# The left and right side projections of a tile issued in turn, product by product, into two PSUM banks

## The reference

```python
u = jnp.einsum('bid,bjd->bij', h, h) / temper
a = jax.nn.softmax(u, axis=-1)
delta = a * adjacency_matrix
attn = delta / (jnp.sum(delta, axis=-1, keepdims=True) + 1e-10)
hl = h @ wl.T + b_l          # "left"
hs = h @ ws.T + b_s          # "self"
hr = h @ wr.T + b_r          # "right"
ctx = einsum(attn * upper, hl) + diag_a[..., None] * hs + einsum(attn * lower, hr)
o = (ctx - mean) / jnp.sqrt(var + LN_EPS) * g + beta
return (jax.nn.relu(o), None)
```

## Time and profile before

| | |
|---|---|
| time, median of 3 runs | 1282.53 us (1281.9 to 1283.6) |
| the profiled execution's own time | 1282.98 us |
| its span, first to last instruction | 1281.2 us |
| TensorE matmul busy | 1263.4 us, 99% |
| TensorE weight loads busy | 1166.7 us, 91% |
| VectorE busy | 990.4 us, 77% |
| ScalarE busy | 632.6 us, 49% |
| GpSimd busy | 370.6 us, 29% |
| mean granted TensorE clock | 0.996 |
| a full step (gram of layer 1 at 606.53 and at 645.56) | 39.03 us |

### The profile page before, as it was taken

The page is one execution under the profiler, slowest core; times in us unless marked ns, Lnnn a source line. Parts: engine busy times, 40 slices in busy tenths (PEclk is TensorE's granted clock), DMA queues, the critical chain, the costliest instruction groups (busy, mean ns, idle before and its releaser), DMA issues.

```text
span 1281.2 us, 34717 instructions
## 1 busy us (share of the span) xinstructions
PE 1263.4 (99%) x13844; PEld 1166.7 (91%) x13844; DVE 990.4 (77%) x2691; ACT 632.6 (49%) x1338; POOL 370.6 (29%) x401
## 2 busy tenths in 40 slices
PE   9999999999999999999999999999999999999986
PEld 8999999999999999999999999999999999999975
DVE  6777778777878777787778787777877777877877
ACT  6544554544554445545445545455454455454543
POOL 3322323232323222323223232223232232323211
PEclk9999999999999999999999999999999999999989
DMA  8211110111110111110111101111101111011000
GB/s 275 85 39 57 58 57 25 35 57 57 57 57 4 55 57 57 57 28 31 57 58 58 57 15 44 57 57 57 43 16 57 57 58 58 20 39 45 26 14 26
DMA packets 53072, 66.34 MB, mean 52 GB/s; under 512 B 17840, under 2 KB 39856, under 8 KB 52784
## 3 DMA queue, kind: packets, MB, share of 16 engines
q1 hardware_dynamic: 52768, 63.93, 16.5%
q10 hardware_dynamic: 144, 0.20, 0.0%
HBM read 38.54 MB, written 12.58 MB: 40 GB/s over the span
## 4 chain that ended last, share of the span: by engine, by line
PE 97%; DVE 1%; issue 1%; ACT 1%; POOL 0%; POOLq 0%; DVEq 0%; ACTq 0%
PE bank L420 25%; PE bank L422 23%; PE bank L421 23%; PE bank L623 7%; PE bank L569 4%; PE bank L532 4%; PE bank L517 3%; PE bank L498 3%; PE bank L545 2%; PE bank L555 2%; PE bank L603 1%; PE bank L631 0%; DVE probs L1222 0%; POOL probs L1727 0%; PE bank L745 0%
## 5 line engine op out<-in xcount | busy, mean ns | idle before, releaser
L420 PE MATMUL bank<-w_hi,hT_hi 128*128 128x384 f32 x1158 | 405.4, 350 | 0.2 <-ACT hT_hi L1048 0.2
L422 PE MATMUL bank<-w_hi,hT_lo 128*128 128x384 f32 x1158 | 390.3, 337 | 0.0
L421 PE MATMUL bank<-w_lo,hT_hi 128*128 128x384 f32 x1158 | 390.1, 337 | 0.0
L420 PEld LDWEIGHTS bank<-w_hi,hT_hi 128*128 128x128 f32 x1158 | 218.3, 189 | 6.6 <-issue 2.0
L421 PEld LDWEIGHTS bank<-w_lo,hT_hi 128*128 128x128 f32 x1158 | 218.9, 189 | 0.0
L422 PEld LDWEIGHTS bank<-w_hi,hT_lo 128*128 128x128 f32 x1158 | 218.3, 189 | 0.0
L1293 DVE TENSOR_TENSOR hlr<-bank,rows 128x384 f32<-128x384 f32 x256 | 142.3, 557 | 70.9 <-PE bank L422 68.0
L1740 POOL TENSOR_TENSOR ln_rstd<-ln_var,minus_half 128x2 f32<-128x2 f32 x125 | 96.2, 769 | 322.1 <-DVE ln_var L1386 113.8
L1727 POOL TENSOR_TENSOR probs<-probs,row_max 128x768 f32<-128x768 f32 x64 | 94.6, 1478 | 265.7 <-DVE row_max L1228 265.7
L1310 DVE TENSOR_TENSOR late<-bank,rows 128x384 f32<-128x384 f32 x128 | 71.3, 558 | 118.0 <-PE bank L422 117.9
L420 PE MATMUL bank<-xT_hi,w_hi 128*128 128x256 f32 x558 | 158.7, 284 | 0.0
(11 more groups left out here) (131 smaller groups left out, 2370.9 us busy)
## 6 DMA issues: line engine op xcount, KB each, us to landing
v_halves<-v_stage SPq DMA_DIRECT2D x128, 99.0 KB, 2.3
x_in<-in_x SPq DMA_DIRECT2D x32, 384.0 KB, 4.0
xT_in<-in_xT SPq DMA_DIRECT2D x31, 384.0 KB, 3.4
out<-late SPq DMA_DIRECT2D x31, 384.0 KB, 2.4
late<-in_w SPq DMA_DIRECT2D x7, 576.0 KB, 6.5
adj_in<-in_adj SPq DMA_DIRECT2D x32, 96.0 KB, 3.8
adjT_in<-in_adjT SPq DMA_DIRECT2D x64, 48.0 KB, 3.2
rows<-in_vectors SPq DMA_DIRECT2D x1, 1536.0 KB, 8.7
```

Source lines behind the costliest of these rows:

```text
L420: nc.tensor.matmul(o, l_hi, r_hi, start=first and n == 0, stop=False)
L421: nc.tensor.matmul(o, l_hi, r_lo, start=False, stop=False)
L422: done = nc.tensor.matmul(o, l_lo, r_hi, start=False, stop=final and n == last)
```

## The change

`project_side` keeps its waits, which move to a function `side_waits` of their own. `project_sides` first does the waits of both sides of a tile, and then issues the 18 matmuls of the tile in turn, left, right, left, right, each pair with the same stationary part of h. The number of matmuls, their operands, their banks and the order of the terms within each side are as before; where two neighbours had different W parts with the same h part they now have different W matrices and banks.

```diff
-            def project_side(st, l, t, m):
+            def side_waits(st, l, t, m):
                 if st.unit(LATE) == 0 and t == 0 and m == LEFT:
...
                 if t == 1 and m == RIGHT:
 
                     need(pe, e_ready, st.count(LATE, 4, 2 * l + 2))
+
+            def project_side(st, l, t, m):
+                side_waits(st, l, t, m)
                 project_h(st, l, t, m, HLR_BANKS[l][2 * t + m]).then_inc(hlr_psum, 1)
 
             def project_sides(st, l):
+
                 for t in range(T):
                     for m in (LEFT, RIGHT):
-                        project_side(st, l, t, m)
+                        side_waits(st, l, t, m)
+                    for kc in range(KC):
+                        h_hi, h_lo = hT_hi[:, t, kc, :], hT_lo[:, t, kc, :]
+                        for n, (a, part) in enumerate(((h_hi, 0), (h_hi, 1), (h_lo, 0))):
+                            for m in (LEFT, RIGHT):
+                                final = kc == KC - 1 and n == 2
+                                done = nc.tensor.matmul(HLR_BANKS[l][2 * t + m][:, 0:D], a,
+                                                        weight(W_LATE + 3 * l + m, kc)[part],
+                                                        start=kc == 0 and n == 0, stop=final)
+                                if final:
+                                    done.then_inc(hlr_psum, 1)
```

## The result

| | before | after |
|---|---|---|
| median | 1282.40 us (4 runs, 1281.9 to 1283.6) | 1295.41 us (4 runs, 1295.2 to 1295.7) |
| span of the profiled execution | 1281.2 us | 1293.8 us |
| a full step | 39.03 us | 39.45 us |

The changed kernel is slower by a ratio of 1.0100, 95% interval 1.0087 to 1.0113, that is 13.0 us. The forecast was 1294.6 us. The step in the table is read at one place; the mean from gram(0) of the second unit to gram(0) of the 31st, 29 steps, is 39.04 us before and 39.44 after.

The account below looks back on a forecast made before the run. TensorE, busy 99% of the span, was taken to bound the kernel. 9.6 + 2.2 + 0.3 = 12.1 us on the profiled 1282.98 us gave 1295.1, median 0.45 lower: 1294.6 us, range 1284 to 1305.

Parts of the forecast that it names:

- The products: TensorE's 2,196 products in `project_sides`: interval stays 173.3 ns despite the new order, so 0 us.
- Layer 1: VectorE gets the left side late, delaying h0; TensorE waits 0.32 us at transpose_h in thirty steps, 9.6 us.
- Layer 0: Right side's wait for the context now stands ahead of slot 1: hole of 0.07 us in 31 stages, 2.2 us.
- The first unit: Where VectorE still splits weights, the new order may add up to 0.4 us once; 0.3 us taken.

Follow-up runs that it names:

- run 5: Changed kernel with both edits, right side's waits ahead of slot 2 and statistics of h0 ahead of the left side: 1283.47 us.
- run 1: Sides take turns in layer 1 only, layer 0 as in the kernel before: 1292.28 us, 9.5 over the kernel before.
- run 4: Changed kernel with VectorE's statistics of h0 in layer 1 moved ahead of the left side: 1286.53 us, 3.8 over the kernel before.
- Run 3: Changed kernel with the right side's waits ahead of its first product, slot 2, no longer ahead of slot 1: 1292.29 us.
- runs 2: Sides take turns in layer 0 only, layer 1 as in the kernel before: 1286.34 us, 3.6 over the kernel before.
- Run 8: Changed kernel with one added, unused VectorE addition ahead of the statistics of h0 in layer 1: 1310.31 us.

## Why the prediction was right

- **The products.** Forecast 0 us in place of a gain. Right: 173.4 ns, and run 5 bounds it at 0.4 ns of cost and 0.7 ns of gain. The Trainium skill (TensorE: Matmul & The Clock Gate, Back-to-back issue gap) gives an isolated gap that comes to 162.5 ns for 384 columns. Neither order reaches it here, with 173.3 and 173.4 ns, so the 11 ns between are not the price of accumulating twice running in one bank; what they are, no run shows.
- **Layer 1.** Forecast 0.32 us a step, 9.6 us. Measured 0.32 us a step and 9.5 us (run 1), with each link where it was forecast. Over all thirty steps the trace's mean is 0.31 us, 9.4 us together. It came from the order of VectorE's list: `stats_outer` stood behind two sides that it does not need (run 4).
- **Layer 0.** Forecast 0.07 us in each of 31 stages, 2.2 us. The trace has 0.09 in 29 of them, 0.16 in the last and none in the first unit, which has no context of a unit before to wait for: 2.7 us. The release took 0.12 us, the upper end of the rows used. Run 3 closes it.
- **The first unit.** Forecast 0.3 us and bounded at 0.4, measured 0.9 from its first gram to its second. Of this, 0.8 lie between its first transpose_e and mix, which are 46.54 - 41.68 = 4.86 us apart, before 45.03 - 40.97 = 4.06. This term was sized too small. TensorE's rows there, first after and then before:

```profile
41.68 0.38 PE L617 MATMUL bank<-ident,e_di 128*128 128x128 f32 x2
46.54 1.53 PE L637 MATMUL bank<-hlr,aT 64*64 64x386 f32 x16 [0.92 <-DVE aT L1314]
```

```profile
40.97 0.38 PE L603 MATMUL bank<-ident,e_di 128*128 128x128 f32 x2
45.03 1.53 PE L623 MATMUL bank<-hlr,aT 64*64 64x386 f32 x16 [0.55 <-DVE aT L1300]
```

I had bounded it by VectorE's late left side alone. VectorE's rows show a second thing, again after and then before:

```profile
39.67 1.83 DVE L1298 SCALAR_TENSOR_TENSOR dz<-z_di,diag 128x2 f32<-128x2 f32 x1
41.43 0.55 DVE L1307 TENSOR_TENSOR hlr<-bank,rows 128x384 f32<-128x384 f32 x1
```

```profile
38.57 0.16 DVE L1284 SCALAR_TENSOR_TENSOR dz<-z_di,diag 128x2 f32<-128x2 f32 x1
38.65 0.55 DVE L1293 TENSOR_TENSOR hlr<-bank,rows 128x384 f32<-128x384 f32 x1
39.11 2.98 DVE L1173 TENSOR_TENSOR w_lo<-late,w_hi 128x1152 fp32r<-128x1152 f32 x1
```

An instruction of 0.16 us takes 1.83 us, and the right side of tile 0 comes behind it. Before, the right side was already out and it was a weight split behind it that was slow (2.98 us; the same split takes 1.34 to 1.68 at its other places in these two traces). In both traces the slow instruction runs beside GpSimd's split of x (39.61 to 41.49 us after, 38.99 to 40.87 before). The six traces with turns in layer 0 (the changed kernel and runs 2, 3, 4, 5 and 8) have `dz` at 1.81 to 1.84 us, the four without have it at 0.16. That GpSimd is the cause, no run shows.

- **What I did not forecast.** Read along the two traces, the span's 12.6 us are 0.6 more before the first gram (it starts at 34.38 us, before at 33.77, and no changed instruction has run by then), 0.9 in the first unit's layer 0, 12.0 in the next 29 stages of layer 0 and in the 30 of layer 1, 0.2 in the step next to last ahead of its layer 1, less 1.1 us that this step gives back (below). I take the 0.6 for chance: the ten traces of all versions have the first gram anywhere from 33.48 to 34.38 us, and the chain of the changed kernel's trace starts with a weight transfer of 7.12 us, the DMA 1% of its page.

So the forecast's 12.1 us was short by 0.6 in the first unit and 0.5 in layer 0, and 0.2 too long in layer 1: 13.0 us for what the change does. That the median too is 13.0 over the kernel before is in part luck, since the 0.6 and the 1.1 us of the single traces are not in the forecast at all and could have fallen otherwise.

## What to carry to other kernels

Issuing two accumulations in turn moves the end of the first one to the end of both, here by 8 products. Where an engine takes the results in a fixed order, everything written behind the first result moves with it, needed or not: compare that delay, less the idle that it swallows, with the cover of the next instruction on the bounding engine, and put what does not need the result ahead of it. Then look at what still stands behind a late result: in run 4 `shift` does, and 0.71 us of the cover are spent. Waits lifted out of a loop are paid as soon as one is met later than the loop's first instruction could start; leave each at its first user.

## What the runs showed of the hardware

A repeated stationary part is loaded again (13,844 loads in both kernels), and neither it nor the change of bank at each product alters the interval: 173.3 ns before, 173.4 after.

In the step next to last, TensorE runs at half its clock for a while after two idle waits (2.3 and 1.4 us). Stretches of it, before and after the change, with the granted clock third from the end of the line:

```profile
1227.80:1231.80 4.00, 4.00 (x15) 4.00 (x14) 2.91 (x10) 0.81 (x4) 0.94 (x1) 0.50 0.00 0
1232.30:1240.00 7.70, 7.70 (x47) 7.16 (x46) 5.53 (x17) 2.97 (x6) 0.69 (x1) 1.00 0.00 0
```

```profile
1241.40:1243.20 1.80, 1.80 (x8) 1.80 (x7) 1.76 (x7) 0.81 (x4) 0.00 (x0) 0.50 0.00 0
1243.60:1250.00 6.40, 6.40 (x40) 5.86 (x39) 4.44 (x15) 2.26 (x4) 1.36 (x2) 1.00 0.00 0
```

At 0.50 (1.2 GHz) a product takes 320 ns in place of 173. The gram ahead of these products runs slow too, so the spell lasted from 1226.3 to about 1232.1 us before and from 1240.0 to about 1243.5 after. In it stand 12 intervals of 320 ns before and 5 after, seven fewer, 7 x 147 ns = 1.0 us; with 0.1 us in the gram that is the 1.1 us that this step gave back. The order of this part is the same in both kernels. In the ten traces there are 5, 5 and 4 such intervals in the changed kernel, run 1 and run 3, and 9 to 13 in the others. Run 8, which has the longest holes ahead of it, has 9, so the length of the spell does not follow that of the holes, and what sets it stays open.
